# A mixture-of-experts kernel: GpSimd's parameter copies moved forward, a front without fillers, one set of transposes moved back

## The reference, cut to what matters

```python
xn = rms_w * (x * rsqrt(mean(x * x) + EPS))
gate = xn @ wg_W + wg_b + (genre_embed @ gg_W + gg_b)
gate_w = softmax(gate)
topk_w, topk_i = top_k(gate_w, 2)
cw = sum(one_hot(topk_i, E) * topk_w[..., None], axis=-2)
h1 = relu(x @ W1[e] + b1[e])          # 256 -> 512
h2 = relu(h1 @ W2[e] + b2[e])         # 512 -> 512
out_e = h2 @ W3[e] + b3[e]            # 512 -> 256
out = x + sum_e cw[e] * out_e
```

## Time and profile before

| | |
|---|---|
| three runs | 470.95, 470.95 and 468.47 us, median 470.95 |
| profiled execution, its own time | 467.62 us |
| its span | 465.9 us |
| PE busy | 426.2 us (91%) |
| POOL busy | 304.9 us (65%) |
| DVE busy, ACT busy | 306.2 us (66%), 288.8 us (62%) |
| mean granted clock of PE | 0.964 |

### The profile page before, as it was taken

How to read it: one execution, slowest core, us unless ns; L and a number is a source line. 1 busy time by engine, 2 the same in 40 slices (tenths; PEclk the granted TensorE clock), 3 DMA queues, 4 the chain that set the end, 5 groups by cost and what they waited for, 6 DMA issues and landing times.

```text
span 465.9 us, 13099 instructions
## 1 busy us (share of the span) xinstructions
PE 426.2 (91%) x4284; PEld 384.2 (82%) x4284; DVE 306.2 (66%) x538; ACT 288.8 (62%) x608; POOL 304.9 (65%) x457
## 2 busy tenths in 40 slices
PE   7607989999989999999999999899999999999990
PEld 6407879988888988998989888799998899898880
DVE  4798775758467667577477577455566767776650
ACT  6603969859388587687786764455554456654450
POOL 5631870877778788787777777778656666564451
PEclk9955899999999999999999999999999999999997
DMA  8989179646435535241342431434223322011121
GB/s 292 353 238 355 60 260 365 203 126 161 125 64 141 132 64 138 40 60 37 53 80 107 59 59 25 70 62 69 47 48 48 49 47 48 26 26 30 24 32 22
DMA packets 27178, 49.46 MB, mean 106 GB/s; under 512 B 8267, under 2 KB 21645, under 8 KB 24941
## 3 DMA queue, kind: packets, MB, share of 16 engines
q0 software_dynamic: 13632, 18.00, 23.6%
q1 hardware_dynamic: 9280, 30.45, 18.2%
q10 hardware_dynamic: 4205, 0.17, 0.5%
HBM read 40.08 MB, written 17.83 MB: 124 GB/s over the span
## 4 chain that ended last, share of the span: by engine, by line
PE 30%; POOL 25%; issue 17%; DMA 10%; DVE 6%; POOLq 5%; ACT 2%; SPq 1%; DVEq 0%; ACTq 0%
PE bank L1270 18%; POOL out L635 7%; DMA out<-area,cto 6%; PE y_banks L1340 6%; POOL area L600 4%; DMA out<-in_x 3%; PE bank L1255 3%; POOL prm L549 2%; POOLq L621 2%; POOL cprm L612 2%; PE bank L1231 1%; POOL expo L494 1%; DVE area L1067 1%; POOL inv_scale L500 1%; POOL cw L623 1%
## 5 line engine op out<-in xcount | busy, mean ns | idle before, releaser
L1270 PE MATMUL bank<-area,w_hi 128*128 128x256 f16 x1536 | 253.8, 273 | 4.9 <-DVE area L1067 4.2
L1270 PE MATMUL bank<-area,w_lo 128*128 128x256 f16 x768 | 209.3, 273 | 0.0
L799 ACT ACTIVATE area<-bank,cprm 128x256 f32<-128x256 f32 (+1 forms) x264 | 131.8, 556 | 66.5 <-PE bank L1270 45.8
L1270 PEld LDWEIGHTS bank<-area,w_hi 128*128 (+1 forms) x1536 | 149.8, 98 | 23.3 <-issue 6.2
L1065 DVE CAST area<-area 128x512 f16<-128x512 f32 (+1 forms) x144 | 65.4, 454 | 126.7 <-ACT area L799 116.4
L635 POOL DMA_INDIRECT out<-area,cto x71 | 119.1, 1678 | 41.0 <-issue 22.5
L1067 DVE TENSOR_TENSOR area<-area 128x512 f16<-128x512 f32 (+1 forms) x144 | 100.7, 700 | 4.9
L600 POOL DMA_INDIRECT area<-x_ext,cfrom x65 | 68.8, 1058 | 38.6 <-POOL cfrom L595 26.3
L1340 PE MATMUL y_banks<-w_hi,area 128*128 (+1 forms) x520 | 90.7, 273 | 0.9 <-DVE area L1067 0.9
L1270 PEld LDWEIGHTS bank<-area,w_lo 128*128 (+1 forms) x768 | 75.1, 98 | 8.7
L809 ACT ACTIVATE area<-area,cw 128x256 f32<-128x256 f32 x71 | 32.2, 499 | 68.8 <-DVE area L1072 48.9
(11 more groups left out here) (203 smaller groups left out, 475.4 us busy)
## 6 DMA issues: line engine op xcount, KB each, us to landing
stage<-in_weights SPq DMA_DIRECT2D x10, 1024.0 KB, 6.8
area<-in_x SPq DMA_DIRECT2D x8, 512.0 KB, 7.3
x_ext<-in_x SPq DMA_DIRECT2D x8, 512.0 KB
out<-in_x SPq DMA_DIRECT2D x8, 512.0 KB, 11.0
w_lo<-in_weights SPq DMA_DIRECT2D x4, 1024.0 KB, 6.4
w_hi<-in_weights SPq DMA_DIRECT2D x2, 1024.0 KB, 4.9
out<-area,cto POOLq DMA_INDIRECT x71
area<-x_ext,cfrom POOLq DMA_INDIRECT x65, 3.3
```

The lines of the kernel that those rows point to most:

```text
L799: ins = act.activation(to[:, m * T + u * wide:m * T + (u + 1) * wide], ps_h[layer][b][:, a * T + u * wide:a * T + (u + 1) * wide], ACT.Rel ...
L1270: ins = nc.tensor.matmul(banks[m // 2][:, (m % 2) * T:(m % 2) * T + wide], weight, xp[:, cols], start=(k == 0 and n == 0), stop=(k == chun ...
```

## The change

Four edits. POOL's step copies the parameters of tile i+3 (into the slot that tile i leaves) right behind the wait for tile i's output, ahead of the wait for the adds before; for tiles by halves behind the adds. The adds now come before `copy_weights(i+2)`, and `parameters(rank)` is the last thing of the step; rank 1's are computed on step 0 instead of 1. In the start of the main part the copies for tiles 1 and 2 stand behind the gathers of tiles 0 to 2. On PE the fillers between the one-hot batches are gone, and `weight_sums(0)` stands ahead of the four spans. On DVE the row numbers of the first tiles are written between the two operations of the first span. On PE the transposes of tile 2 stand behind layer three of tile 0; all others stay.

```diff
-LOWS_AT, ..., PARAMETERS_AT = {1: 2, 2: 3}, {}, {0: 1}, {0: 2, 1: 3}, {1: 1}
+LOWS_AT, ..., PARAMETERS_AT = {1: 2, 2: 3}, {}, {0: 1}, {0: 2, 1: 3}, {0: 1}
...
+            def next_parameters(i, s):
+                if i + RING == PAIRED_AT:
+                    pool.wait_ge(s_wsq, 4 * E)
+                if i + RING < TILES:
+                    experts_of.append(copy_parameters(i + RING, s))
             def step(i, s, first=False, late=None, next2=True, next4=True):
-                if i + 2 == PAIRED_AT:
-                    pool.wait_ge(s_wsq, 4 * E)
-                if next2:
-                    experts = copy_parameters(i + 2, s2)
                 copy_columns(cto[:, s, :], tab_to, i, s_idx)
                 if next4:
                     gather_next(i + 1, s1)
...
-                if late is not None:
-                    link(parameters(late))
                 if not by_halves(i):
                     pool.wait_ge(s_y, 2 * i + 3)
                     pool.sem_inc(s_own, 1)
+                    next_parameters(i, s)
                 if first:
                     pool.wait_ge(s_out0, OUT_PARTS * 16)
                 else:
                     pool.wait_ge(s_add, i * SUB * 16)
                     pool.sem_inc(s_own, 1)
+                add_rows(i, s)
+                if by_halves(i):
+                    next_parameters(i, s)
                 if next2:
-                    copy_weights(i + 2, s2, experts)
-                add_rows(i, s)
+                    copy_weights(i + 2, s2, experts_of[i + 2])
+                if late is not None:
+                    link(parameters(late))
...
-                if i < 2:
-                    experts_of.append(copy_parameters(i, i))
+                    experts_of.append(copy_parameters(0, 0))
+            for i in range(1, RING):
+                experts_of.append(copy_parameters(i, i))
...
                 ins.then_inc(s_inv, 1)
-                keep_busy(WARM_BATCH, ones16[:, :], bank[3])
+            weight_sums(0)
             for r in range(2 * J // SPAN):
                 pe.wait_ge(s_hotc, r + 1)
...
                 ins.then_inc(s_late, 1)
-                if r == SUMS_BEHIND_SPAN:
-                    weight_sums(0)
...
-            later_half_columns(0)
-            dve.wait_ge(s_inv, BATCHES)
-            dve.tensor_scalar(tab_from[:, 0:EARLY], ps_early, ...).then_inc(s_from, 1)
-            for r in range(1, 2 * J // SPAN):
-                later_half_columns(r)
+            def early_rows():
+                dve.wait_ge(s_inv, BATCHES)
+                dve.tensor_scalar(tab_from[:, 0:EARLY], ps_early, ...).then_inc(s_from, 1)
+            for r in range(2 * J // SPAN):
+                later_half_columns(r, between=early_rows if r == 0 else None)
...
-                if next2:
+                if next2 and i > 0:
                     transpose_x(i + 2, (s + 2) % RING, turn + (s + 2) // RING + 1)
                 if two(i):
                     layer3_pair(i, w)
                 else:
                     layer3(i, w)
+                if i == 0:
+                    transpose_x(i + 2, (s + 2) % RING, turn + (s + 2) // RING + 1)
```

More of the change, by code:

```diff
@@ L82 @@
 BEFORE = [max([p for p in range(q) if PLACE[p] == PLACE[q]], default=None) for q in range(CHUNKS)]
-LOWS_AT, SQUARES_AT, SUMS_AT, HIGHS_AT, PARAMETERS_AT = {1: 2, 2: 3}, {}, {0: 1}, {0: 2, 1: 3}, {1: 1}
+LOWS_AT, SQUARES_AT, SUMS_AT, HIGHS_AT, PARAMETERS_AT = {1: 2, 2: 3}, {}, {0: 1}, {0: 2, 1: 3}, {0: 1}
 for rank in range(FRONT, E):
@@ L94 @@
 SPAN = 2 * BATCH
-SUMS_BEHIND_SPAN = 0
 EARLY = 8
@@ L100 @@
 WARM_START = 24
-WARM_BATCH = 4
 WARM_TILES = 16
@@ L1022, in _, with later_half_columns @@
                                   ALU.is_equal).then_inc(s_hot, 1)
-            def later_half_columns(r):
+            def later_half_columns(r, between=None):
                 span = slice(r * SPAN, (r + 1) * SPAN)
@@ L1029, in later_half_columns @@
                                        .to_broadcast(late), ALU.is_equal))
+                if between is not None:
+                    between()
                 dve.tensor_tensor(hot_c[:, r], hot_c[:, r], values[:, span].rearrange("p (g n) -> p g n", n=RUN)
                                   .unsqueeze(2).to_broadcast(late), ALU.mult).then_inc(s_hotc, 1)
-            later_half_columns(0)
-            dve.wait_ge(s_inv, BATCHES)
-            dve.tensor_scalar(tab_from[:, 0:EARLY], ps_early, float(N // 2), None, ALU.add).then_inc(s_from, 1)
-            for r in range(1, 2 * J // SPAN):
-                later_half_columns(r)
+            def early_rows():
+                dve.wait_ge(s_inv, BATCHES)
+                dve.tensor_scalar(tab_from[:, 0:EARLY], ps_early, float(N // 2), None, ALU.add).then_inc(s_from, 1)
+            for r in range(2 * J // SPAN):
+                later_half_columns(r, between=early_rows if r == 0 else None)
             def tables():
```

## The result

The changed kernel takes 464.53 us (median of 4 runs, 463.99 to 465.12), the kernel before 470.41 (4 runs, 468.47 to 470.95). The ratio is 0.988, interval 0.985 to 0.992. The forecast was 464.0 us. Run again beside other runs of the kernel before (experiment 5), the ratio was 0.986 (0.983 to 0.990). The profiled execution took 464.45 us, 3.17 less than the one of before (467.62). One of the ten executions of experiment 1 took 1571.81 us and one of the four of experiment 10 took 482.96: the medians given there include them, the ratios leave them out.

The account below looks back on a forecast made before the run. PE sets the pace with POOL close behind, reaching PE through three waits. From the profiled 467.62, less 4.67 (stalls) and 0.95 (front), 462.0; plus 2.0 for timed runs, 464.0 us. Range 460.4 to 469.7.

Parts of the forecast that it names:

- The three stalls: PE's late starts of layer two at tiles 4, 6 and 21, behind ACT waiting for POOL's parameter copies: -4.67 us.
- The free 2.35 us of ACT's delay: An ACT wait for a parameter copy of some 2.35 us costs PE nothing; only the excess is paid.
- The copy of tile 7: POOL's tightest parameter copy in the new order, starting at 128 where ACT wants it at 131.8.
- The margin of 5.2 us: Tile 7's parameter copy: 2.8 us ahead of ACT's need, which with the free 2.35 makes 5.2 us.
- rival B: POOL becomes the bound: x us more per three steps costs 5.5 x less 5.2; at x = 3, 475.3 us; chance 0.11.
- The front: Before layer one of tile 0: `x_high(0)` starts at 50.85 instead of 51.79, -0.95 us, bounds -1.6 and -0.35.
- the 1.31 us before the row numbers: In the front's one-hot batches: with fillers PE ended 1.31 us behind DVE.
- rival C: Without batch fillers the clock stays at 1.2 GHz up to layer two of tile 0: 5.7 us extra, 469.7; chance 0.09.
- Tile 2's transposes: Moved behind layer three of tile 0: -0.5 us there, lost again at tile 1; net 0, bounds -0.5 and +0.5.
- The tiles by halves: Last steps: only the order inside a pair of adds changes and PE waits for DVE, not POOL: 0.
- From 462.0 to 464.0: 2.0 us added, the middle, because the three timed runs stand 0.85 to 3.33 us above the profiled execution.

Follow-up runs that it names:

- experiment 5: The changed kernel run again without edit, beside the kernel before: 462.07 us, ratio 0.986.
- experiment 1: The kernel before run again without edit, for a second trace: 468.26 us, ratio 1.000.
- experiment 10: Version 4 with POOL copying parameters four times instead of once on tiles 3 to 27: 477.84 us, ratio 1.023.
- experiment 2: POOL's new order alone; fillers, weight sums, row numbers and tile 2's transposes as in the kernel before: 462.08 us, ratio 0.987.
- (3): The kernel before with only the front's edits of PE and DVE; POOL's order and tile 2's transposes as before: 465.74 us, ratio 0.996.
- (11): The kernel before with one edit, tile 1's parameter copy behind the gathers of tiles 1 and 2: 468.23 us, ratio 1.000.
- (9): Version 4 with POOL copying parameters twice on tiles 3 to 27, 25 copies more: 460.75 us, ratio 0.983.
- version 4: The changed kernel with tile 2's transposes put back ahead of layer three: 460.67 us, ratio 0.983.
- (6): Version 4 with the four fillers behind each one-hot batch put back: 462.75 us, ratio 0.988.
- (7): Version 4 with the weight sums put back behind the first span: 460.78 us, ratio 0.983.
- (8): Version 4 with 4 instead of 16 fillers ahead of the transposes of tile 0: 461.35 us, ratio 0.985.
- (12): Version 4 with weight sums behind the first span and 8 instead of 16 fillers ahead of tile 0's transposes: 462.77 us, ratio 0.988.

## Why the prediction was right, point by point

**The three stalls**, -4.67: right, -4.68 in the trace (1.02, 2.14, 1.52), and experiment 2, which has only POOL's order, reaches a ratio of 0.987, where the whole change reaches 0.988 (0.986 in experiment 5). This was the main term and it carries the result. How firmly each stall stands differs: the one at tile 4 also goes with the front alone (3) and with the order at the start of the main part alone (11); the one at tile 21 went only with POOL's new order in the steps.

**The free 2.35 us of ACT's delay**: agrees. The three waits left in the changed kernel are 1.2 us each, and PE has no gap behind them. A wait of 3.07 us in experiments 1, 3 and 11 left a gap of 0.49, which with the 0.17 of modelled tail is 0.66: 2.4 us were free there.

**The copy of tile 7**: forecast near 128, it ran at 126.74. The margin of 5.2 us was put too small, and it was the margin of the wrong thing. Doubling the copy on 25 tiles cost nothing (9). With four copies it was the gather of the next tile that came late (10): gathers stand ahead of the wait for the output in POOL's step, and the prediction never asked what else a late POOL delays. The sum 5.5 x - 5.2 of rival B fails with it: it gave about 5 us of loss for one extra copy, and none was there. For three extra copies, x = 5.4, it gives 24.5 us; the profiled executions of 10 and 4 differ by 13.9. So if its form is right, the margin was nearer 16 us (an estimate from these two).

**The front**, -0.95: -0.91 in the trace, by the steps that were named. Row numbers 4.99 us behind the first batch (6.80 before), sums held by ACT's squares for 1.18 us, ACT idle for 0.89 ahead of `x_high(0)`, since PE now is late. That it came so near is in part luck. From the first batch to the transposes of tile 1 the kernels without these edits took 23.33 (before), 23.34 (1), 23.80 (2) and 23.83 (11), those with them 22.42 (the changed kernel), 22.04 (5), 22.96 (3) and 22.94 (4): -0.37 to -1.29 against the first trace, by the moment at which the clock rose and, in 4, a wait of 0.31 for gather 0. The prediction's bounds, -1.6 and -0.35, hold. One row was misread: the 1.31 us before the row numbers are DVE's idle time behind its span operation; PE ended its small matmuls 2.6 us behind DVE's last batch (44.05 against 41.45). The sum did not use it. Nor is the front a term by itself. Alone it gave 2.0 us in the median (3): the copy of x to the output is asked for 3.3 us sooner (the prediction had 1.9), POOL starts its adds sooner, and two of the stalls shrink. Front and POOL's order overlap there, as the traces show. The medians are too coarse to show it: together (version 4) they gave 7.1, alone 5.7 and 2.0, each with an interval of 1.1 to 1.7 us to either side.

**The clock** (rival C): it did not come true. The rival expected a later rise without the fillers; over all traces it was not later than with them. It rose at 50.4 in the changed kernel, 0.5 us later than in the trace of before against the first batch's 0.43, and the spread between executions is wider than that (below).

**Tile 2's transposes**, 0 with -0.5 to +0.5: 0.19 in the comparison of the two traces (-0.50 and +0.69), 1.14 as an edit of its own (4), outside the bounds. The step that failed is "PE stood idle 1.58 us before them, for gather 2", taken as something only this edit could remove. The change itself issues gather 2 ahead of the copies and sooner besides, at 55.08 instead of 58.93, so the wait was gone anyway.

**The tiles by halves**, 0: small shifts of up to 0.9 us in favour (a stall of 0.85 us at 407.82, in the step of tile 31, is gone in the changed kernel and in every version with POOL's new order), and ACT's stall of one execution against it.

**From 462.0 to 464.0**: the 2.0 us had no reason, and that they fit is luck. The sum against the profiled execution was 5.62 us, the measured difference of the two profiled executions 3.17. Of the 2.45 us between them 0.43 is the later start, 1.72 the stall at tile 31, 0.19 tile 2, the rest small. Experiment 1 shows what was missing: the trace of before was one of an early front, the other comes 2.1 us later to the same point. Had this been read as a lag of POOL, the forecast would have been too low. The 2.0 were added for the distance between the profiled execution and the timed ones, but the changed kernel's profiled execution (464.45) lies among its timed ones (463.99 to 465.12), and 1.72 us of it are a stall that its second trace does not have. On that second occasion the kernel took 462.07 us, 1.9 below the forecast. What was forecast well is the difference: 5.6 us by the sum, 5.9 and 6.6 between the medians.

## What to carry to other kernels

A helper engine with little idle time can be the bound through one early wait: look for the waits that reach the main engine, sum only the excess over what its buffers absorb, and move what others wait for ahead of what nobody waits for. When two edits both remove the same wait, price each with the other already made. Ask of a late engine for every thing it hands out which comes late first, not only for the one that is late now.

## What the runs showed of the hardware that was not expected

TensorE's clock rose from 1.2 to 2.4 GHz at moments that differ between executions by almost 5 us, and fillers in the batches did not bring it sooner. Read from the slices of 1 us and counted from the first batch, it rose with fillers at 12.6 (before), 12.6 (1), 15.6 (2), 13.4 (6) and 15.0 (11), without them at 12.7 (the changed kernel), 13.7 (3), 12.9 (4), 11.7 (5), 11.4 (7), 11.4 (8), 10.8 (9), 11.2 (10) and 13.5 (12). From the span's start this is 48.0 (9) to 52.9 (11). During the batches it was 0.50 in all of them. What sets the moment no experiment isolates. In version 2 the spans, the fillers and the transposes behind them still ran at half speed. Its busy times by stretch (us; PE, PE's weight loads, DVE, ACT and POOL, each with its count, then the granted clock, the DMA share and GB/s) show it, with the granted clock at 0.50 in the one slice and the rise inside the next.

```profile
51.00:52.00 1.00, 1.00 (x9) 0.94 (x8) 0.00 (x0) 0.60 (x1) 0.82 (x6) 0.50 0.00 0
52.00:53.00 1.00, 1.00 (x15) 1.00 (x14) 0.28 (x1) 1.00 (x2) 0.69 (x5) 0.66 0.00 0
```

In the middle of the kernel the clock fell once: from 1.00 to 0.50 behind PE's wait of 3.04 us in experiment 10. From 243 on it was 1.00 again.

POOL's busy time told little of how much room it had. In the window of the earlier trace rows it was busy 25.64 us before, 27.27 in version 4 and 26.13 with the copies doubled (9), at the same 33.12 us of PE. Over the whole span it was busy 309.8 us in version 4 and 313.5 in 9, whose 25 extra copies alone took 13.4 us: other operations became shorter, such as the copy of the row numbers `cto`, 865 ns in the mean in version 4 and 650 in 9. The length of an operation changes with its place in the order: the parameter copy takes 583 ns in the mean after the change and took 1079 before, while the copy of the gate weights went from 233 to 851 as it took the place behind the adds. What beside them stretches them no run isolates. So an engine that seemed to keep pace just so had room for one more copy a tile, and not for three.
